# A vision-transformer layer with a matrix exponential: the count of squarings taken from the third and fourth powers

## The chip, the cores and the metric

The kernel runs on one core of one Trainium2 chip. The metric is the time of one execution on the device in microseconds (us), as the median of several runs. Its engines are named as in the profile: PE (TensorE), PEld (its weight load), DVE (VectorE), ACT (ScalarE), POOL (GpSimd), SP (SyncE, which here only issues DMAs).

## What is computed

32 images of 96x96 become 38 tokens of 256 features each (1216 rows). One attention layer with 16 heads follows, and then a feed-forward block with a mixture of experts. In the block, `expm` is the matrix exponential; its three arguments, the generators, are 256x256 and antisymmetric:

```python
logits = xn @ moe_gate_w + moe_gate_b
topw, topi = jax.lax.top_k(logits, K)             # K = 2 of E = 8 experts
h = _gelu(jnp.einsum('bsd,edh->ebsh', xn, ew1) + eb1[:, None, None, :])
eo = jnp.einsum('ebsh,ehd->ebsd', h, ew2) + eb2[:, None, None, :]
moe_out = jnp.einsum('ebsd,bse->bsd', eo, w_dense)
for i in range(NROT):                             # NROT = 3
    moe_out = moe_out @ expm(gens[i])
```

The entries of `gens` in the inputs are 8 x 0.5 x 0.02 x (g - g transposed) with g of unit normals, so their spread is 0.113. The largest sum of absolute values over a row or column of the three, worked out from the inputs, is 26.53.

## The kernel before, in words

The rows are cut into 11 tiles of 114 (three images each; the last has 76). Embedding, the projections and attention run tile by tile. Behind them a router gives every row its two experts, and the pairs of row and expert are packed into 26 slots of 128 rows, one expert to a slot. Then come the slots, and at the end a gather of the results with the last rotation, gate and store per tile.

**A slot j.** The program of each engine goes through the slots in a fixed order, written out by hand.

- POOL gathers the slot's 128 rows from memory by an indirect DMA into one of two buffers (`gather`, L445), and scatters the results (`scatter`, L450). Its loop (L465) runs: wait until the rows of slot j+2 are transposed, `gather(j+4)`, `scatter(j)` once DVE has written the results of slot j, then side work: a scale at L471 for j below 11, an add at L478 for j from 2 to 12, two diagonal matrices at L485 for j from 12 to 22.
- PE's loop (L1438) runs for slot j: `expert_of(j)` (a register loaded from SBUF), `turn_xs(j+2)` (transposes of the gathered rows, L1409), `hidden(j+1)` (first expert layer, L1422), at most one piece of the exponential, and `project(j)` (second layer, L1431).
- ACT evacuates the transposes (L624) and applies Gelu (L635). DVE adds the bias (`slot_step`, L1097) and so frees the bank for `project(j+2)` and starts `scatter(j)`. SP loads the first layer's weights, 512 KB a slot, three slots ahead (L322).

**The exponential.** `scale_generators` (L897, DVE) takes s as the larger of `SQUARINGS` = 4 and the exponent of (largest column sum of absolute values / 1.7), and multiplies the generators by 2^-s. PE makes the second, third and fourth powers of the three of them (`product`, L1362, evacuated by ACT at L603), and the transposes of the fourth (L1369, evacuated at L618). DVE builds a polynomial of degree 12 less the identity: `poly_first` (L1056) for generators 0 and 1 ahead of slot 0 and for 2 in slot 0, `poly_second` in slots 1 to 3 and `poly_third` in slots 4 to 6, each with a product of PE between. It is then squared s times: `turn_square` (four transposes), ACT's copy `keep_YT` (L648), `product`, and DVE's `square` (L1079, 2Y + Y squared). A loop behind slot 7 (`MORE_AT`) squares all three `more` = s - 3 times, and slots 8 to 16 (`SQ_AT`) carry one squaring each, which are the last three of every generator. In slots 17 and 19 (`E_AT`) the three results are multiplied together (`second`, `third`). The counts are set by one line:

```python
P0_AT, P1_AT, MORE_AT, SQ_AT, E_AT = 1, 4, 7, 8, (17, 19)
```

`link` on DVE puts a wait on each instruction's own completion behind it. `more` is loaded from SBUF into a register of PE at L1403, of ACT at L644 and of DVE at L1086, all ahead of slot 0.

Of the kernel before, what the change touches and what calls it, by code (L numbers as in the profile page):

```python
# [13 lines left out]
B, SEQ, D = 32, 38, 256  # L14
# [16 lines left out]
G = 3  # L31
SQUARINGS = 4
# [13 lines left out]
NCONST = 840  # L46
# [4 lines left out]
def vit_kernel(nc, patches, w_tok, w_qkv, w_o, w_pre, w1, w2, b2, gens, gens_t,  # L51
# [6 lines left out]
    with ctx:  # L58
# [3 lines left out]
        def sem(name):  # L62
            return ctx.enter_context(nc.semaphore(name))
# [64 lines left out]
        nrmi_sb = sb("nrmi_sb", 5, i32)  # L128
# [82 lines left out]
        var_set, root_set = sem("var_set"), sem("root_set")  # L211
        z_bounded = sem("z_bounded")
# [55 lines left out]
        P0_AT, P1_AT, MORE_AT, SQ_AT, E_AT = 1, 4, 7, 8, (17, 19)  # L268
# [220 lines left out]
        def _(act):  # L489
# [154 lines left out]
            more = act.value_load(nrmi_sb[0:1, 4:5], min_val=1, max_val=17)  # L644

# [8 lines left out]
            for j in range(NS - 2):  # L654
                keep_xsT(j + 2, j % 2)
                u = j - SQ_AT
                if 0 <= u < 3 * G:
                    keep_YT(3 * more + u + 1, u % G, 0)
                if j in E_AT:
                    n = E_AT.index(j)  # L660
                    act.wait_ge(e_turned, n + 1)
                    nc.scalar.activation(YT[n], bank[0][:, :], ACT.Copy).then_inc(e_evac, 1)
                gelu(j + 1, (j + 1) % 2, expert_of(j + 1))
                if j == 0:
                    act.wait_ge(d_z, 16 * NT)
                    nc.scalar.activation(h_sb[0:T, :].rearrange("p (t d) -> p t d", d=D),
                                         v_sb[0:T, 0:NT * PW].rearrange("p (t d) -> p t d", d=PW)[:, :, 0:D], ACT.Gelu).then_inc(abel_set, 1)
                if j == MORE_AT:
                    with act.Fori(0, more) as i:
                        for n in range(G):  # L670
                            keep_YT(3 * i + n + 1, n, MORE_BANK[n])
# [20 lines left out]
        def _(dve):  # L692
# [204 lines left out]
            def scale_generators():  # L897
# [6 lines left out]
                link(nc.vector.tensor_scalar(nrmi_sb[:, 4:5], nrmi_sb[:, 2:3], 1.0 - SQUARINGS, None, ALU.add))  # L904
# [136 lines left out]
            dve.wait_ge(n_scaled, 2)  # L1041
            c = [1.0]
            for k in range(1, 13):
                c.append(c[-1] / k)
# [26 lines left out]
            def poly_third(n):  # L1071
                stt(Y[n], A2[n], c[2], A[n])
                stt(Y[n], A3[n], c[3], Y[n])
                dve.wait_ge(p_made, G + n + 1)
                nc.vector.tensor_tensor(Y[n], Y[n], bank[0][:, :], ALU.add).then_inc(y_set, 1)
# [10 lines left out]
            more = dve.value_load(nrmi_sb[0:1, 4:5], min_val=1, max_val=17)  # L1086
# [36 lines left out]
            for j in range(NS):  # L1123
# [5 lines left out]
                if 0 <= u < 3 * G:  # L1129
                    square(3 * more + u + 1, u % G, 0)  # L1130
# [37 lines left out]
        def _(pe):  # L1168
# [234 lines left out]
            more = pe.value_load(nrmi_sb[0:1, 4:5], min_val=1, max_val=17)  # L1403

# [33 lines left out]
            for j in range(NS):  # L1438
# [3 lines left out]
                if 0 <= u < 3 * G:  # L1442
                    pe.wait_ge(s_kept_cr, 3 * more + G + u)
                    turn_square(bank[0], Y[u % G]).then_inc(s_turned, 1)
                if j in E_AT:
                    if j == E_AT[0]:
                        pe.wait_ge(s_kept_cr, 3 * more + 4 * G)
                    else:
                        pe.wait_ge(e_kept, 1)
                    turn_square(bank[0], Y[0]).then_inc(e_turned, 1)  # L1450
# [12 lines left out]
                if 0 <= u < 3 * G:  # L1463
# [7 lines left out]
                if j == MORE_AT:  # L1471
                    pe.wait_ge(y_set, G)
                    with pe.Fori(0, more) as i:
# [49 lines left out]
def _constants():  # L1523
# [13 lines left out]
    con[TLAST:, K_INV + NT - 1] = 100.0  # L1537
    con[:, K_SEG:K_SEG + E * NT] = (np.arange(E * NT) % NT != 0)
# [63 lines left out]
```

## Time and profile before

| | |
|---|---|
| median of 3 runs | 394.57 us (394.08 to 399.01) |
| the profiled execution | 394.72 us, its span 392.7 us |
| mean granted clock of PE over the span | 0.951 of full |
| PE, DVE, ACT, POOL busy | 88%, 55%, 45%, 39% |

The span runs from the first to the last instruction of the profiled execution; 2.0 us of its time lie outside. Start times in rows count from the start of the span.

### The profile page before, as it was taken

The numbers are of one execution on the slowest core, as the hardware profiler recorded it, in microseconds if no ns is written. First come the engines' busy times: TensorE is split into PE (matmuls) and PEld (weight loads), VectorE is DVE, ScalarE is ACT, GpSimd is POOL, SyncE is SP. The second block draws the span as 40 slices with busy tenths as digits, with TensorE's granted clock in tenths as the row PEclk, the third lists the DMA queues.
The fourth block names the chain that finished last, engine by engine and source line by source line (L and its number), as shares of the span: only waits on it lengthen the run. The fifth ranks groups of instructions, "written<-read, shape, count | busy, mean of one in ns | idle before, by whom it ended". The sixth has DMA issues, their size and how long they took to land.

```text
span 392.7 us, 6931 instructions
## 1 busy us (share of the span) xinstructions
PE 345.1 (88%) x2080; PEld 293.1 (75%) x2080; DVE 214.8 (55%) x581; ACT 178.5 (45%) x423; POOL 151.4 (39%) x168
## 2 busy tenths in 40 slices
PE   2998999769899999679986999999999999794894
PEld 2786454469788888556865899989999999693793
DVE  0237368797999999868785458421221123100175
ACT  1000354588998897335224844334434434341231
POOL 1002804050754663711041447653547446642000
PEclk9999899968999999969989999999999999989599
DMA  8741411133111100274222645523443444531442
GB/s 268 269 140 44 188 58 55 54 97 114 46 48 47 46 33 2 93 335 156 84 69 80 181 121 154 163 93 88 149 149 106 149 151 156 151 103 47 144 144 86
DMA packets 20544, 45.76 MB, mean 117 GB/s; under 512 B 2150, under 2 KB 12836, under 8 KB 20260
## 3 DMA queue, kind: packets, MB, share of 16 engines
q1 hardware_dynamic: 17732, 37.78, 29.1%
q0 software_dynamic: 2496, 6.82, 5.2%
q10 hardware_dynamic: 288, 0.81, 0.7%
q8 instruction: 14, 0.23, 0.3%
q14 instruction: 14, 0.11, 0.1%
HBM read 38.18 MB, written 7.22 MB: 116 GB/s over the span
## 4 chain that ended last, share of the span: by engine, by line
PE 75%; DVE 10%; issue 7%; DMA 3%; ACT 2%; POOL 1%; DVEq 0%; ACTq 0%; POOLq 0%; SPq 0%
PE banks L1422 11%; PE banks L1362 11%; PE banks L1431 10%; PE banks L1205 5%; PE banks L1175 5%; PE banks L1282 5%; PE banks L1258 4%; PE banks L1491 3%; PE banks L1300 3%; PE banks L1333 3%; PE banks L1501 2%; PE banks L1245 2%; PE banks L1191 2%; PE banks L1210 2%; PE banks L1231 2%
## 5 line engine op out<-in xcount | busy, mean ns | idle before, releaser
L1422 PE MATMUL banks<-qn_sb,w_sb 128*128 128x128 f32 x416 | 51.6, 278 | 1.0 <-ACT qn_sb L624 1.0
L624 ACT ACTIVATE qn_sb<-banks,col_sb 128x128 f32<-128x128 f32 x52 | 21.1, 458 | 66.1 <-PE banks L1409 66.1
L1431 PE MATMUL banks<-w_sb,sq_sb 128*128 x208 | 50.0, 385 | 0.3 <-ACT sq_sb L635 0.3
L1422 PEld LDWEIGHTS banks<-qn_sb,w_sb 128*128 128x128 f32 x416 | 49.2, 194 | 1.3 <-ACT qn_sb L624 1.2
L452 POOL DMA_INDIRECT y_rows<-pT_sb,sidx_sb x26 | 26.0, 999 | 56.7 <-DVE pT_sb L1097 55.5
L1431 PEld LDWEIGHTS banks<-w_sb,sq_sb 128*128 128x128 f32 x208 | 39.7, 194 | 5.7 <-issue 0.5
L1097 DVE TENSOR_TENSOR pT_sb<-banks,p_sb 128x256 f32<-128x256 f32 x26 | 11.0, 425 | 51.0 <-PE banks L1431 48.3
L635 ACT ACTIVATE sq_sb<-banks,col_sb 128x128 f32<-128x128 f32 x104 | 32.6, 369 | 12.9 <-PE banks L1422 10.8
L1175 PE MATMUL banks<-wtok_sb,patch_sb 128*114 128x256 f32 x132 | 30.4, 393 | 7.1 <-DMA wtok_sb<-in_w_tok 7.0
L446 POOL DMA_INDIRECT qn_sb<-z_rows,gidx_sb x26 | 27.4, 1054 | 21.1 <-PE banks L1409 14.1
L1175 PEld LDWEIGHTS banks<-wtok_sb,patch_sb 128*114 128x114 f32 x132 | 24.3, 186 | 12.8 <-DMA patch_sb<-in_patches 6.9
L541 ACT ACTIVATE kc_sb<-banks,col_sb 32x152 f32<-32x152 f32 x66 | 31.1, 471 | 2.6 <-PE banks L1245 1.5
L1079 DVE SCALAR_TENSOR_TENSOR p_sb<-p_sb,banks 128x512 f32<-128x512 f32 x12 | 8.3, 688 | 35.6 <-PE banks L1362 35.6
L829 DVE TENSOR_SCALAR kc_sb<-banks,col_sb 32x152 f32<-32x152 f32 x66 | 25.5, 423 | 3.7 <-PE banks L1245 3.2
L1362 PE MATMUL banks<-p_sb,wtok_sb 128*128 128x256 f32 x112 | 26.2, 380 | 0.0
L259 POOL TENSOR_TENSOR qn_sb<-qk_sb,wtok_sb 114x768 f32<-114x768 f32 x11 | 16.4, 1497 | 22.0 <-DVE wtok_sb L786 22.0
L411 POOL TENSOR_TENSOR att_sb<-p_sb 114x256 f32<-114x256 f32 x11 | 8.1, 738 | 41.8 <-DVE p_sb L864 41.8
L1205 PE MATMUL banks<-wqkv_sb,xT_sb 128*114 128x512 f32 x44 | 22.5, 635 | 0.2 <-ACT xT_sb L500 0.2
L1362 PEld LDWEIGHTS banks<-p_sb,wtok_sb 128*128 128x128 f32 x112 | 20.4, 190 | 2.3
L1258 PE MATMUL banks<-kc_sb,qd_sb 96*114 96x76 f32 x176 | 22.0, 274 | 0.0
L1258 PEld LDWEIGHTS banks<-kc_sb,qd_sb 96*114 96x114 f32 x176 | 22.0, 196 | 0.0
L532 ACT ACTIVATE qd_sb<-banks,col_sb 32x304 f32<-32x304 f32 x33 | 19.7, 598 | 4.1 <-PE banks L1231 3.8
(204 smaller groups left out, 668.8 us busy)
## 6 DMA issues: line engine op xcount, KB each, us to landing
w_sb<-in_w SPq DMA_DIRECT2D x26, 512.0 KB
w_sb<-in_w SPq DMA_DIRECT2D x1, 4096.0 KB, 12.6
patch_sb<-in_patches SPq DMA_DIRECT2D x11, 342.0 KB, 3.0
vrep_sb<-v_rows SPq DMA_DIRECT2D x33, 114.0 KB
qk_sb<-y_rows SPq DMA_DIRECT2D x10, 228.0 KB
v_rows<-v_sb SPq DMA_DIRECT2D x11, 114.0 KB
z_rows<-h_sb SPq DMA_DIRECT2D x11, 114.0 KB
out_rows<-h_sb SPq DMA_DIRECT2D x10, 114.0 KB
```

Source lines behind the costliest of these rows:

```text
L446: pool.indirect_dma_start(out=xs_sb[:, s * D:(s + 1) * D], out_offset=None, in_=z_dram, in_offset=bass.IndirectOffsetOnAxis(ap=gidx_sb[:, ...
L452: pool.indirect_dma_start(out=y_dram, out_offset=bass.IndirectOffsetOnAxis(ap=sidx_sb[:, j:j + 1], axis=0), in_=ys_sb[:, s * D:(s + 1) * D ...
L541: last = nc.scalar.activation(kc[:, :, a, :], bank[2][r, :].rearrange("p (n m) -> p n m", m=128)[:, :, c], ACT.Identity, scale=col_sb[r, C ...
L624: last = nc.scalar.activation(xsT_sb[:, (2 * s + c) * 128:(2 * s + c + 1) * 128], bank[1][:, c * 128:(c + 1) * 128], ACT.Identity, scale=c ...
L635: last = nc.scalar.activation(hidT_sb[:, s * HID + c * 128:s * HID + (c + 1) * 128], bank[2 + 2 * s + c // 2][:, (c % 2) * 128:(c % 2 + 1) ...
L829: last = nc.vector.tensor_scalar(kc[:, :, a, :], bank[3][r, :].rearrange("p (n m) -> p n m", m=128)[:, :, c], col_sb[r, C_GK + a:C_GK + a ...
L1175: last = nc.tensor.matmul(bank[2 + slot % 2][0:T, 0:D], patch_sb[:, (slot * FK + k) * T:(slot * FK + k + 1) * T], wtok_sb[:, k * D:(k + 1) ...
L1205: last = nc.tensor.matmul(bank[4 + s][0:T, :], xT_sb[:, (2 * s + k) * T:(2 * s + k + 1) * T], wqkv_sb[:, k * 3 * D:k * 3 * D + 2 * D], sta ...
L1258: last = nc.tensor.matmul(bank[4 + hf][0:T, n * 2 * SEQ:(n + 1) * 2 * SEQ], qd_sb[0:96, q0:q0 + T], kc_sb[0:96, k0:k0 + 2 * SEQ], start=Fa ...
L1362: last = nc.tensor.matmul(dst[:, m * D:(m + 1) * D], xT[:, k * D + m * 128:k * D + (m + 1) * 128], y[:, k * D:(k + 1) * D], start=(k == 0) ...
L1422: last = nc.tensor.matmul(bank[2 + 2 * s + c // 2][:, (c % 2) * 128:(c % 2 + 1) * 128], w1_sb[:, w0:w0 + 128], xsT_sb[:, (2 * s + k) * 128 ...
L1431: last = nc.tensor.matmul(bank[6 + s][:, 0:D], hidT_sb[:, s * HID + k * 128:s * HID + (k + 1) * 128], w2_sb[:, ds(e * 4 * D + k * D, D)], ...
```

## The change

It sets `SQUARINGS` to 2, so s stays what the column sums give if that is above 2. When the third and fourth powers are in SBUF, DVE sums the absolute values of their rows (six reductions of 128x512) and compares the largest of each with eight bounds, (1.7 / 2^q) to the third and to the fourth for q = 1 to 8. In slot 0, behind `turn_xs(2)`, PE multiplies the 16 comparisons with a matrix of ones, so that every partition has the counts over all 128. From them DVE takes t, the number of q for which neither power has a row at or over its bound, but at most s - 2, sets `more` = s - 2 - t + 1, and makes the coefficients of the polynomial as running products of 2^t / k. The polynomial is then that of 2^t times the scaled generator, which leaves s - t squarings: `more` of them in the loop, and one per generator in the slots. All of this comes before `poly_first(0)`. The pieces sit in other slots: `poly_second` in 2 to 4, `poly_third` in 5 to 7 (with one more DVE operation each), the loop behind slot 9, single squarings in slots 10 to 12, the products of the three in 14 and 16. `more` is now loaded into PE's and ACT's registers just ahead of the loop, and into DVE's ahead of `poly_first(0)`. The constants grow from 420 KB to 440 KB.

```diff
@@ -29,7 +29,8 @@
 EPS = 1e-5
 NEG = -1e30
 G = 3
-SQUARINGS = 4
+SQUARINGS = 2
+SHRINK = 8
 THETA = 1.7
 EXPM_LIMIT = 3.925724783138660 * 2.0 ** 17
 
@@ -43,7 +44,8 @@
 K_ID, K_MASK, K_LOW, K_ONE, K_IOTA, K_INV, K_SEG = 0, 128, 256, 384, 512, 640, 662
 K_TILE, K_ROW, K_DUMP = 750, 794, 795
 K_IMG, K_HEAD = 821, 824
-NCONST = 840
+K_RECIP, K_ZERO, K_BOUND = 840, 852, 864
+NCONST = 880
 NPART = 3
 Y_ROWS = 2 * NT * T + NS * 128
 
@@ -125,7 +127,8 @@
         wt_sb = sb("wt_sb", 4 * NT)
         z_sb = sb("z_sb", 4 * NT)
         nrm_sb = sb("nrm_sb", 16)
-        nrmi_sb = sb("nrmi_sb", 5, i32)
+        nrmi_sb = sb("nrmi_sb", 8, i32)
+        al_sb = sb("al_sb", 80)
 
         def tri(t_, k, w):
             return t_[0:T, ds(k * w, w)]
@@ -209,6 +212,7 @@
         x_made, x_kept, x_turned, x_evac, p_made, y_set = (
             sem("x_made"), sem("x_kept"), sem("x_turned"), sem("x_evac"), sem("p_made"), sem("y_set"))
         var_set, root_set = sem("var_set"), sem("root_set")
+        bound_set, counted, more_set = sem("bound_set"), sem("counted"), sem("more_set")
         z_bounded = sem("z_bounded")
         poly_set, stats_done = sem("poly_set"), sem("stats_done")
         s_made, s_kept_cr, s_turned, s_evac = sem("s_made"), sem("s_kept_cr"), sem("s_turned"), sem("s_evac")
@@ -265,7 +269,7 @@
             return not isinstance(t, int) or t >= n
 
         EARLY = 4
-        P0_AT, P1_AT, MORE_AT, SQ_AT, E_AT = 1, 4, 7, 8, (17, 19)
+        P0_AT, P1_AT, MORE_AT, SQ_AT, E_AT = 2, 5, 9, 10, (14, 16)
         MORE_BANK = (0, 4, 5)
 
         block = ctx.enter_context(nc.Block())
@@ -641,8 +645,6 @@
                 keep_xsT(j + 2, s)
                 gelu(j + 1, 1 - s, expert_of(j + 1))
 
-            more = act.value_load(nrmi_sb[0:1, 4:5], min_val=1, max_val=17)
-
             def keep_YT(done, n, b):
                 act.wait_ge(s_turned, done)
                 nc.scalar.activation(YT[n], bank[b][:, :], ACT.Copy).then_inc(s_evac, 1)
@@ -654,7 +656,7 @@
             for j in range(NS - 2):
                 keep_xsT(j + 2, j % 2)
                 u = j - SQ_AT
-                if 0 <= u < 3 * G:
+                if 0 <= u < G:
                     keep_YT(3 * more + u + 1, u % G, 0)
                 if j in E_AT:
                     n = E_AT.index(j)
@@ -666,6 +668,8 @@
                     nc.scalar.activation(h_sb[0:T, :].rearrange("p (t d) -> p t d", d=D),
                                          v_sb[0:T, 0:NT * PW].rearrange("p (t d) -> p t d", d=PW)[:, :, 0:D], ACT.Gelu).then_inc(abel_set, 1)
                 if j == MORE_AT:
+                    act.wait_ge(more_set, 1)
+                    more = act.value_load(nrmi_sb[0:1, 4:5], min_val=1, max_val=19)
                     with act.Fori(0, more) as i:
                         for n in range(G):
                             keep_YT(3 * i + n + 1, n, MORE_BANK[n])
@@ -901,7 +905,6 @@
                 link(nc.vector.tensor_scalar(nrmi_sb[:, 0:1], nrm_sb[:, 8:9].bitcast(i32), 23, None, ALU.logical_shift_right))
                 link(nc.vector.tensor_scalar(nrmi_sb[:, 1:2], nrmi_sb[:, 0:1], -126.0, float(SQUARINGS), ALU.add, ALU.max))
                 link(nc.vector.tensor_scalar(nrmi_sb[:, 2:3], nrmi_sb[:, 1:2], 20.0, None, ALU.min))
-                link(nc.vector.tensor_scalar(nrmi_sb[:, 4:5], nrmi_sb[:, 2:3], 1.0 - SQUARINGS, None, ALU.add))
                 link(nc.vector.tensor_scalar(nrmi_sb[:, 3:4], nrmi_sb[:, 2:3], -1.0, 127.0, ALU.mult, ALU.add))
                 link(nc.vector.tensor_scalar(nrm_sb[:, 9:10].bitcast(i32), nrmi_sb[:, 3:4], 23, None, ALU.logical_shift_left))
 
@@ -1038,10 +1041,32 @@
             nc.vector.tensor_scalar(R[3], R[0], 1.0, None, ALU.add).then_inc(hbs_set, 1)
 
 
-            dve.wait_ge(n_scaled, 2)
-            c = [1.0]
-            for k in range(1, 13):
-                c.append(c[-1] / k)
+            sums, top2 = al_sb[:, 0:12], al_sb[:, 12:14]
+            over, bad, tau = al_sb[:, 16:32], al_sb[:, 32:40], al_sb[:, 51:52]
+            c = [None] + [al_sb[:, 64 + k:65 + k] for k in range(12)]
+            for k, P in enumerate((A3, A4)):
+                for n in range(G):
+                    dve.wait_ge(x_kept, (k + 1) * G + n + 1)
+                    link(nc.vector.tensor_reduce(sums[:, 6 * k + 2 * n:6 * k + 2 * n + 2], P[n].rearrange("p (n c) -> p n c", c=D),
+                                                 AX.X, ALU.add, apply_absolute_value=True))
+            link(nc.vector.tensor_reduce(top2, sums.rearrange("p (k q) -> p k q", k=2), AX.X, ALU.max))
+            nc.vector.tensor_tensor(over.rearrange("p (k q) -> p k q", k=2), top2.unsqueeze(2).broadcast_to([128, 2, SHRINK]),
+                                    con_sb[:, K_BOUND:K_BOUND + 2 * SHRINK].rearrange("p (k q) -> p k q", k=2),
+                                    ALU.is_ge).then_inc(bound_set, 1)
+            dve.wait_ge(counted, 1)
+            link(nc.vector.tensor_reduce(bad, bank[0][:, 0:2 * SHRINK].rearrange("p (k q) -> p q k", k=2), AX.X, ALU.add))
+            link(nc.vector.tensor_scalar(bad, bad, 0.5, 1.0, ALU.is_ge, ALU.mult))
+            link(nc.vector.tensor_reduce(al_sb[:, 48:49], bad, AX.X, ALU.add))
+            link(nc.vector.tensor_scalar(al_sb[:, 48:49], al_sb[:, 48:49], -1.0, float(SHRINK), ALU.mult, ALU.add))
+            link(nc.vector.tensor_copy(nrmi_sb[:, 5:6], al_sb[:, 48:49]))
+            link(nc.vector.tensor_scalar(nrmi_sb[:, 6:7], nrmi_sb[:, 2:3], -float(SQUARINGS), None, ALU.add))
+            link(nc.vector.tensor_tensor(nrmi_sb[:, 5:6], nrmi_sb[:, 5:6], nrmi_sb[:, 6:7], ALU.min))
+            link(nc.vector.tensor_tensor(nrmi_sb[:, 6:7], nrmi_sb[:, 6:7], nrmi_sb[:, 5:6], ALU.subtract))
+            nc.vector.tensor_scalar(nrmi_sb[:, 4:5], nrmi_sb[:, 6:7], 1.0, None, ALU.add).then_inc(more_set, 1)
+            link(nc.vector.tensor_scalar(nrmi_sb[:, 7:8], nrmi_sb[:, 5:6], 127.0, None, ALU.add))
+            link(nc.vector.tensor_scalar(tau.bitcast(i32), nrmi_sb[:, 7:8], 23, None, ALU.logical_shift_left))
+            link(nc.vector.tensor_scalar(al_sb[:, 52:64], con_sb[:, K_RECIP:K_RECIP + 12], tau, None, ALU.mult))
+            link(nc.vector.tensor_tensor_scan(al_sb[:, 64:76], al_sb[:, 52:64], con_sb[:, K_ZERO:K_ZERO + 12], 1.0, ALU.mult, ALU.add))
             eye = con_sb[:, K_ID:K_ID + 128]
 
             def stt(out_, in0, k, in1):
@@ -1069,7 +1094,8 @@
                 add_eye(poly[n], c[4])
 
             def poly_third(n):
-                stt(Y[n], A2[n], c[2], A[n])
+                link(nc.vector.tensor_scalar(Y[n], A[n], c[1], None, ALU.mult))
+                stt(Y[n], A2[n], c[2], Y[n])
                 stt(Y[n], A3[n], c[3], Y[n])
                 dve.wait_ge(p_made, G + n + 1)
                 nc.vector.tensor_tensor(Y[n], Y[n], bank[0][:, :], ALU.add).then_inc(y_set, 1)
@@ -1083,7 +1109,8 @@
                 link(nc.vector.tensor_tensor_reduce(att_sb[0:T, 0:D], h_sb[0:T, t * D:(t + 1) * D], row_sb[0:T, R_GW:R_GW + D],
                                                     1.0, row_sb[0:T, R_GCB:R_GCB + 1], ALU.mult, ALU.add, z_sb[0:T, t:t + 1]))
 
-            more = dve.value_load(nrmi_sb[0:1, 4:5], min_val=1, max_val=17)
+            dve.wait_ge(more_set, 1)
+            more = dve.value_load(nrmi_sb[0:1, 4:5], min_val=1, max_val=19)
             dve.wait_ge(d_b, 16)
 
             def expert_of(j):
@@ -1126,7 +1153,7 @@
                 if P1_AT <= j < P1_AT + G:
                     poly_third(j - P1_AT)
                 u = j - SQ_AT
-                if 0 <= u < 3 * G:
+                if 0 <= u < G:
                     square(3 * more + u + 1, u % G, 0)
                 if j == E_AT[0]:
                     second()
@@ -1400,8 +1427,6 @@
             pe.wait_ge(experts_set, 1)
             pe.wait_ge(where_set, 1)
             pe.wait_ge(x_evac, G)
-            more = pe.value_load(nrmi_sb[0:1, 4:5], min_val=1, max_val=17)
-
             def turn_xs(j, s, turn):
                 pe.wait_ge(d_xs[s], 16 * (turn + 1))
                 pe.wait_ge(xsT_set, j)
@@ -1439,12 +1464,16 @@
                 u, e = j - SQ_AT, expert_of(j)
                 if j + 2 < NS:
                     turn_xs(j + 2, j % 2, j // 2 + 1)
-                if 0 <= u < 3 * G:
+                if j == 0:
+                    pe.wait_ge(bound_set, 1)
+                    nc.tensor.matmul(bank[0][:, 0:2 * SHRINK], con_sb[:, K_ONE:K_ONE + 128], al_sb[:, 16:32], start=True,
+                                     stop=True).then_inc(counted, 1)
+                if 0 <= u < G:
                     pe.wait_ge(s_kept_cr, 3 * more + G + u)
                     turn_square(bank[0], Y[u % G]).then_inc(s_turned, 1)
                 if j in E_AT:
                     if j == E_AT[0]:
-                        pe.wait_ge(s_kept_cr, 3 * more + 4 * G)
+                        pe.wait_ge(s_kept_cr, 3 * more + 2 * G)
                     else:
                         pe.wait_ge(e_kept, 1)
                     turn_square(bank[0], Y[0]).then_inc(e_turned, 1)
@@ -1460,7 +1489,7 @@
                     if n:
                         pe.wait_ge(y_set, n)
                     product(bank[0], A4T[n], poly[n]).then_inc(p_made, 1)
-                if 0 <= u < 3 * G:
+                if 0 <= u < G:
                     pe.wait_ge(s_evac, 3 * more + u + 1)
                     product(bank[0], YT[u % G], Y[u % G]).then_inc(s_made, 1)
                 if j in E_AT:
@@ -1470,6 +1499,8 @@
                 project(j, j % 2, e)
                 if j == MORE_AT:
                     pe.wait_ge(y_set, G)
+                    pe.wait_ge(more_set, 1)
+                    more = pe.value_load(nrmi_sb[0:1, 4:5], min_val=1, max_val=19)
                     with pe.Fori(0, more) as i:
                         for n in range(G):
                             pe.wait_ge(s_kept_cr, 3 * i + n + 1)
@@ -1535,6 +1566,9 @@
     con[:, K_ROW] = p
     con[:, K_DUMP:K_DUMP + NS] = 2 * NT * T + 128 * np.arange(NS) + p[:, None]
     con[TLAST:, K_INV + NT - 1] = 100.0
+    con[:, K_RECIP:K_RECIP + 12] = 1.0 / np.arange(1, 13)
+    for n in range(2):
+        con[:, K_BOUND + n * SHRINK:K_BOUND + (n + 1) * SHRINK] = (THETA / 2.0 ** np.arange(1, SHRINK + 1)) ** (n + 3)
     con[:, K_SEG:K_SEG + E * NT] = (np.arange(E * NT) % NT != 0)
     return con
 
```

## Rows read from the trace of the kernel before

**Rows 1.** The page, its head and the busy time of the engines.

```profile
span 392.7 us, 6931 instructions
...
PE 345.1 (88%) x2080; PEld 293.1 (75%) x2080; DVE 214.8 (55%) x581; ACT 178.5 (45%) x423; POOL 151.4 (39%) x168
```

**Rows 2.** Busy time by windows; behind the engines PE's clock, DMA share, GB/s.

```profile
320.00:340.00 20.00, 20.00 (x131) 18.42 (x130) 5.91 (x14) 9.36 (x27) 11.56 (x16) 1.00 0.49 150
```

**Rows 3.** Timeline, PE's `turn_xs` at the head of slots 9, 17, 20 and 21.

```profile
270.17 0.38 PE L1409 MATMUL banks<-con_sb,qn_sb 128*128 128x128 f32 x2
...
317.35 0.38 PE L1409 MATMUL banks<-con_sb,qn_sb 128*128 128x128 f32 x2
...
332.88 0.38 PE L1409 MATMUL banks<-con_sb,qn_sb 128*128 128x128 f32 x2
...
336.62 0.38 PE L1409 MATMUL banks<-con_sb,qn_sb 128*128 128x128 f32 x2
```

**Rows 4.** The instructions of L1079 (durations ns min/median/max).

```profile
L1079 DVE SCALAR_TENSOR_TENSOR p_sb<-p_sb,banks x12: 686/689/690, 260.2 to 315.8; 128x512 f32<-128x512 f32 x12
```

**Rows 5.** Chain that ended last, ahead of slot 0: start, length, what.

```profile
210.38 1.11 issue
```

**Rows 6.** Timeline of PE, `turn_xs(2)` in slot 0.

```profile
216.12 0.41 PE L1409 MATMUL banks<-con_sb,qn_sb 128*128 128x128 f32 x2 [0.99 <-ACT qn_sb L624]
```

**Rows 7.** The instructions of L792, a reduction of 128x512.

```profile
L792 DVE TENSOR_REDUCE nrm_sb<-p_sb x3: 668/676/677, 63.5 to 69.6; 128x2 f32<-128x512 f32 x3
```

**Rows 8.** Timeline of ACT: the last evacuation of a fourth power.

```profile
208.31 0.60 ACT L603 ACTIVATE qk_sb<-banks 128x512 f32<-128x512 f32 x1 [1.13 <-PE banks L1362]
```

**Rows 9.** Timeline of DVE: first and last of eleven linked 128x1 operations.

```profile
162.63 0.15 DVE L900 TENSOR_SCALAR nrm_sb<-nrm_sb 128x1 f32<-128x1 f32 x1
...
164.52 0.16 DVE L911 TENSOR_TENSOR nrm_sb<-nrm_sb 128x1 f32<-128x1 f32 x1
```

**Rows 10.** Timeline of DVE: `poly_first` of 0 and 1, then `slot_step(0)`.

```profile
205.56 0.43 DVE L1058 TENSOR_SCALAR qk_sb<-patch_sb 128x512 f32<-128x512 f32 x1 [1.55 <-ACT qk_sb L603]
...
211.69 0.29 DVE L1053 SCALAR_TENSOR_TENSOR qk_sb<-con_sb,qk_sb 128x128 f32<-128x128 f32 x1
220.74 0.42 DVE L1097 TENSOR_TENSOR pT_sb<-banks,p_sb 128x256 f32<-128x256 f32 x1 [8.75 <-PE banks L1431]
```

**Rows 11.** Timeline of POOL: `scatter(0)`, L471, `gather(5)`, and L471 in slot 1.

```profile
221.45 1.01 POOL L452 DMA_INDIRECT y_rows<-pT_sb,sidx_sb  x1 [3.19 <-DVE pT_sb L1097]
222.51 1.10 POOL L471 TENSOR_SCALAR hb_sb<-h_sb,rr_sb 114x256 f32<-114x256 f32 x1
223.78 1.28 POOL L446 DMA_INDIRECT qn_sb<-z_rows,gidx_sb  x1 [0.17 <-issue]
...
229.72 0.57 POOL L471 TENSOR_SCALAR hb_sb<-h_sb,rr_sb 114x256 f32<-114x256 f32 x1
```

**Rows 12.** Busy time by windows behind `gather(5)`, columns as in rows 2.

```profile
227.80:228.30 0.50, 0.50 (x5) 0.47 (x4) 0.33 (x1) 0.25 (x2) 0.00 (x0) 1.00 0.00 0
```

**Rows 13.** Timeline of PE: `turn_xs(5)` at the head of slot 3.

```profile
231.34 0.38 PE L1409 MATMUL banks<-con_sb,qn_sb 128*128 128x128 f32 x2
```

**Rows 14.** Timeline of DVE: `slot_step(19)` behind `third`.

```profile
335.20 0.42 DVE L1097 TENSOR_TENSOR pT_sb<-banks,p_sb 128x256 f32<-128x256 f32 x1 [0.84 <-DVE ywide_sb L1117]
```

**Rows 15.** Chain that ended last, around slot 22.

```profile
338.27 4.80 DMA qn_sb<-z_rows,gidx_sb
...
343.56 2.56 PE banks L1422 x16
346.12 2.61 PE banks L1431 x8
...
348.95 1.79 PE banks L1422 x16
```

**Rows 16.** Waits of PE in the slots: in total, times, longest.

```profile
PE banks L1409 <- DMA qn_sb<-z_rows,gidx_sb: 2.6, 1, 2.6
```

**Rows 17.** Busy time by windows behind that wait, columns as in rows 2.

```profile
344.00:347.00 3.00, 3.00 (x16) 2.82 (x15) 0.00 (x0) 1.66 (x6) 1.48 (x3) 0.56 0.30 81
```

## The prediction

> **What bounds the kernel now.** I read the page first: PE is busy for 88% of the span [rows 1]. A share over the whole span doesn't say what bounds the slots, where the change lies, so the windows come next. From 320 to 340 us PE is busy for all 20.00 us at full clock, while DVE has 5.91 and ACT 9.36 [rows 2]. So in the slots PE's work is the time. The timeline gives its size by the starts of `turn_xs`: from slot 9 to slot 17 it is 47.18 us for 8 slots with a squaring, 5.90 each; slot 20 carries no piece and takes 3.74 [rows 3]. A squaring of one generator thus costs PE 2.16. L1079 ran 12 times [rows 4]: four squarings of three generators, so s was 4 and `more` 1.
>
> Then the waits. In the slots PE waits once for a gather, 2.6 us [rows 16]. The chain around it shows why: DVE is late with `slot_step(19)` because `third` stands ahead of it and a register load follows, 0.84 idle [rows 14], so POOL is late with `scatter(19)` and with the gather behind it, which takes 4.80 from issue to landing [rows 15]. That line DVE, scatter, gather, PE is what the change can hit a second time. At the start, PE idles in pieces, and DVE sits idle for 8.75 us ahead of `slot_step(0)` [rows 10], which is cover for new work there.
>
> **How many squarings go.** The inputs give it. The largest column sum is 26.53, over 1.7 it is 15.6, so s stays 4 under the new minimum of 2. I worked out the powers of gens/16: the largest row sum of absolute values is 0.0524 in the third and 0.00914 in the fourth. The bounds are 0.0768 and 0.0326 at q = 2, and 0.0096 and 0.0020 at q = 3. So t = 2, which is also the cap s - 2. `more` is 1 again and one squaring per generator is left in slots: 2 instead of 4. Six squarings of one generator go: 6 x 2.16 = 13.0 us, all of it PE time in a stage where PE is never idle.
>
> **What comes back at the start.** Step by step in the time of the profile:
> - PE's load of `more` ahead of slot 0 goes. The chain has 1.11 "issue" there [rows 5]; about 1.0 of it should go. `turn_xs(2)` then starts at 216.12 - 1.0 = 215.1 [rows 6].
> - The reductions: six at 0.68 [rows 7]. DVE is free from about 204; the three over third powers are through by 206.1, the last over a fourth waits for its evacuation at 208.31 + 0.60 [rows 8] and ends at 209.6, the comparison by 210.1. PE asks for it at 215.3. That wait costs nothing, with 5 us to spare. DVE's idle 8.75 hides it.
> - The matrix product with ones is 128x16, which no row shows. Between nothing and a transpose pair (0.38, rows 6's kind); I take 0.2, and DVE sees it at 215.8.
> - Now 13 small operations in a chain. Linked 128x1 operations start (164.52 - 162.63)/10 = 0.19 apart [rows 9]: 2.5 us, to 218.3. Then DVE loads `more`, 0.8 by rows 14, to 219.1. In the kernel before these stood in idle time; here they lie on the line.
> - `poly_first` for two generators: from 205.56 to 211.98 it took 6.42 [rows 10]. The scalars now come from SBUF; I take the same price, and 10% more (0.6) as its other end. It ends at 225.5. Another register load shows with about 0.5: `slot_step(0)` starts at 226.0 instead of 220.74.
> - `scatter(0)` started 0.71 behind that, `gather(5)` 2.33 behind the scatter [rows 10, 11]: 229.0. In the kernel before, all packets had landed by 227.8 [rows 12], so that gather took at most 4.0; 3.5 is my estimate, 4.80 [rows 15] the upper end. It lands at 232.5.
> - PE needs it for `turn_xs(5)` at the head of slot 3. By then PE has done slots 0 to 2 with only one product of a polynomial (before: two), so it is there at about 228.4. It waits some 4 us, until 232.6. Before, slot 3 began at 231.34 [rows 13]. That is 1.3 later, and one product of 1.73 more is still owed (5.46 a slot with one product, less 3.74): 3.0 lost.
>
> `project(2)` needs `slot_step(0)` done, at 226.4; it comes to it at about 226.7. `poly_second(0)` is through at about 233, its product is due at 234.6. Nothing else is late on this line.
>
> **Smaller edits.** L471 behind `scatter(0)` took 1.10 while DVE was in the same kind of work, against 0.57 in slot 1 [rows 11]. I keep the long one; the short one would give 0.5 back. The Trainium skill (GPSIMD Engine Reference, section "1. Specifications") says that GpSimd contends with VectorE instructions of two SBUF inputs, of which `poly_first(2)` is made; by the rule the term stays, without it the sum would be 385.9.
> One DVE operation less in `scale_generators` gives 0.2. `poly_third` has one more per generator, 0.46, inside slots of 5.46 in which DVE has some 3.5: nothing, 1.4 without that cover. The register load ahead of the loop, in mid-work of all engines: PE loads one such register in every slot and slot 20 shows no gap, so nothing, 1.1 (rows 5) at most. ACT has the time until the first transposes of the loop. ACT loses six copies and DVE six operations, off the path. 20 KB more constants: nothing to 0.1.
> `third` now stands in slot 16, followed by slots without a piece as before: the same late scatter, the same wait of 2.6 and the same half clock, now at slot 19. But seven slots instead of four follow it, three of them still with side work on POOL: I add 0.2.
>
> **The sum.** -13.0 + 3.0 + 1.7 - 0.2 + 0.2 = -8.3. The profiled execution took 394.72, so 386.4. It stands 0.15 over the median, which makes no difference.
>
> **The rivals.**
> - *The line at the start isn't late.* If DVE's chain or the gather were some 4 us shorter, slot 3 begins without a wait: -13.0 - 1.0 + 0.2 = -13.8, that is 380.9. For it: 8.75 idle on DVE. Against: 6.42 of `poly_first` was done within that idle time's lead, and now all of it comes behind PE's product at 215.8.
> - *The wait comes, the clock stays.* 384.7. For it: the granted clock is held over the pieces of idle time around slot 0. Against: rows 15 to 17.
> - *The gathers bind more.* `gather(5)` takes 4.80: 1.3 later. And in slots 19 to 22 the ring from the end of slot j to `turn_xs(j+5)` is 0.3 (PE to DVE) + 0.71 + 1.0 + 1.2 + 0.2 + 4.8 = 8.2 against two slots of 3.74: 0.7 for every three slots, 1.2 in all with a part of a third. 386.4 + 2.5 = 388.9. For it: the 4.80 was in just such slots. Against: the half clock lengthens these slots and gives POOL time.
> - *The count doesn't shrink.* If the comparison finds a row over the bound at q = 1 (a fault in the count, or rounding far beyond the factor of 1.4 that I find between sum and bound), `more` is 3 and all 12 squarings stay, most in the loop. Then only the losses remain: 3.0 + 1.7 + 0.2 = +4.9, 399.6, slower than before. It decides at t: with t = 1 three squarings remain, -6.5 + 4.7 = -1.8; only t = 0 is slower. For it: a count over two engines in fp32. Against: the margins above.
>
> **How the numbers follow.** Forecast 386.4 with a chance of 0.45, the wait without the clock 0.2, late gathers 0.2, no wait 0.1, no shrinking 0.05. The range reaches from 381.5 (most of the case without a wait) to 390.5 (late gathers with the bounds of 0.6 for scalars and 1.1 for the register load). A measurement of this kernel can tell some 2%, 7.9 us, from no change; that is at 386.7, just over my forecast. Half of the forecast's share, most of the next and all of the case without a wait lie beyond it: faster 0.50, within 2% 0.47, slower 0.03 (the part of the last case that measures over 2%).
>
> **What would show it.** L1079 with 6 instructions, and slots 10 to 12 at 5.90. A wait of PE for a gather at slot 3 of 3 to 5 us, and one at slot 19 of 2.6. DVE's `slot_step(0)` some 10 us behind the matrix product with ones. A granted clock near 0.5 behind both waits. I'm wrong if `turn_xs(5)` finds its gather landed, if L1079 has other than 6, or if `bound_set` holds PE in slot 0.

## The result, and the profile after

| | before | after |
|---|---|---|
| median | 394.82 us (4 runs, 394.08 to 399.01) | 383.95 us (4 runs, 383.07 to 385.58) |
| profiled execution, span | 394.72, 392.7 | 384.60, 382.7 |
| granted clock of PE | 0.951 | 0.955 |

The ratio of after to before is 0.9708, with a 95% interval of 0.9631 to 0.9785: faster. Some executions of a program run at a lower granted clock and take over 1.5% longer than its fastest one; the ratios in this document leave them out. In a later set the same two programs gave 0.9742 (0.9696 to 0.9788). The forecast was 386.4, range 381.5 to 390.5; from profile to profile it was -8.3, and -10.1 was measured.

The head of the page after, its answer to [rows 1], and the instructions of the squaring (L1079 is now L1105):

```profile
span 382.7 us, 6792 instructions
...
PE 332.1 (87%) x2010; PEld 280.3 (73%) x2010; DVE 223.6 (58%) x598; ACT 175.5 (46%) x417; POOL 152.8 (40%) x168
```
```profile
L1105 DVE SCALAR_TENSOR_TENSOR p_sb<-p_sb,banks x6: 686/687/689, 272.8 to 293.0; 128x512 f32<-128x512 f32 x6
```

Six squarings are left of [rows 4]'s twelve, and PE's busy time fell by 13.0 us. The timeline of PE has `turn_xs` (now L1434) at the heads of slots 0 and 3 and the matmuls of `project(2)` (L1456); of DVE the first and last of the count's small operations (L1057, L1069), the first and last of `poly_first` for 0 and 1 and `slot_step(0)` (L1124):

```profile
215.85 0.41 PE L1434 MATMUL banks<-con_sb,qn_sb 128*128 128x128 f32 x2 [0.99 <-ACT qn_sb L628]
...
228.56 1.99 PE L1456 MATMUL banks<-w_sb,sq_sb 128*128 x8 [0.74 <-DVE pT_sb L1124]
...
234.29 0.44 PE L1434 MATMUL banks<-con_sb,qn_sb 128*128 128x128 f32 x2 [3.74 <-DMA qn_sb<-z_rows,gidx_sb]
```
```profile
216.43 0.17 DVE L1057 TENSOR_REDUCE al_sb<-banks 128x8 f32<-128x16 f32 x1 [5.83 <-PE banks L1469]
...
218.70 0.18 DVE L1069 TENSOR_TENSOR_SCAN al_sb<-al_sb,con_sb 128x12 f32<-128x12 f32 x1
...
219.93 0.49 DVE L1083 TENSOR_SCALAR qk_sb<-patch_sb,al_sb 128x512 f32<-128x512 f32 x1 [1.04 <-issue]
...
226.73 0.35 DVE L1078 SCALAR_TENSOR_TENSOR qk_sb<-con_sb,al_sb,qk_sb 128x128 f32<-128x128 f32 x1
227.87 0.42 DVE L1124 TENSOR_TENSOR pT_sb<-banks,p_sb 128x256 f32<-128x256 f32 x1 [0.79 <-issue]
```

The reader sees the predicted line: DVE idles 5.83 us until PE's product with ones, and from there everything is in a row, so `slot_step(0)` comes 7.13 us later than in [rows 10]. The chain that ended last goes on from it through POOL:

```profile
228.59 1.01 POOL y_rows L456
229.64 1.07 POOL hb_sb L475
230.89 3.36 DMA qn_sb<-z_rows,gidx_sb
234.29 0.44 PE banks L1434 x2
```

and the windows behind the wait at slot 3 and behind that at slot 19 have the clock at its full level (the eighth column), where [rows 17] had 0.56:

```profile
234.00:238.00 4.00, 3.71 (x25) 3.47 (x26) 3.06 (x7) 2.06 (x6) 2.75 (x4) 1.00 0.21 66
323.00:326.00 3.00, 3.00 (x23) 2.89 (x24) 0.17 (x1) 1.58 (x5) 2.67 (x4) 1.00 0.62 231
```

At slot 19 the wait is 1.43 where [rows 16] had 2.6: the gather before it took 3.62 us where [rows 15] had 4.80. Slots 20 and 21 (326.66 to 330.83, then to 334.77) take 4.17 and 3.94 instead of 3.74:

```profile
319.21 3.62 DMA qn_sb<-z_rows,gidx_sb
```
```profile
322.87 0.44 PE L1434 MATMUL banks<-con_sb,qn_sb 128*128 128x128 f32 x2 [1.43 <-DMA qn_sb<-z_rows,gidx_sb]
...
326.66 0.38 PE L1434 MATMUL banks<-con_sb,qn_sb 128*128 128x128 f32 x2
...
330.83 0.44 PE L1434 MATMUL banks<-con_sb,qn_sb 128*128 128x128 f32 x2 [0.27 <-issue]
...
334.77 0.44 PE L1434 MATMUL banks<-con_sb,qn_sb 128*128 128x128 f32 x2
...
338.56 0.38 PE L1434 MATMUL banks<-con_sb,qn_sb 128*128 128x128 f32 x2
```

The accounts close on these heads. Slot 3 began at 231.34 [rows 13] and begins at 234.29: 2.95 lost. From there to the last `turn_xs` (slot 23) it was 348.57 - 231.34 = 117.23 and is 338.56 - 234.29 = 104.27: 12.96 won. That is 12.96 of squarings, less 1.73 for the product that is still owed, plus 1.18 of shorter wait, plus 1.65 of clock, less 1.1 in small pieces (below). 2.95 - 12.96 = -10.0, as the spans have it; the last 0.1 of the 10.1 lies outside the span.

### The profile page after: what moved, and what is told of

Its sections match the earlier page's. It is cut to its first block, busy times and chain, and to the rows that moved or that the text cites. A ratio compares the mean times of both kernels' runs of the same rounds, so it can differ in the third digit from the quotient of the medians.

```text
span 382.7 us, 6792 instructions
## 1 busy us (share of the span) xinstructions
PE 332.1 (87%) x2010; PEld 280.3 (73%) x2010; DVE 223.6 (58%) x598; ACT 175.5 (46%) x417; POOL 152.8 (40%) x168
## 4 chain that ended last, share of the span: by engine, by line
PE 71%; DVE 13%; issue 7%; DMA 4%; ACT 2%; POOL 1%; DVEq 1%; POOLq 0%; ACTq 0%; SPq 0%
PE banks L1447 10%; PE banks L1456 9%; PE banks L1389 8%; PE banks L1232 5%; PE banks L1202 5%; PE banks L1309 5%; PE banks L1285 4%; PE banks L1522 3%; PE banks L1327 3%; PE banks L1360 3%; PE banks L1532 3%; PE banks L1272 2%; PE banks L1218 2%; PE banks L1237 2%; PE banks L1258 2%
## 5 line engine op out<-in xcount | busy, mean ns | idle before, releaser
L1456 PE MATMUL banks<-w_sb,sq_sb 128*128 x208 | 49.2, 380 | 0.8 <-DVE pT_sb L1124 0.7
L1456 PEld LDWEIGHTS banks<-w_sb,sq_sb 128*128 128x128 f32 x208 | 38.4, 190 | 6.0 <-issue 1.4
L1124 DVE TENSOR_TENSOR pT_sb<-banks,p_sb 128x256 f32<-128x256 f32 x26 | 11.0, 424 | 47.5 <-PE banks L1456 25.3
L450 POOL DMA_INDIRECT qn_sb<-z_rows,gidx_sb x26 | 28.7, 1103 | 20.1 <-PE banks L1434 13.2
L1309 PEld LDWEIGHTS banks<-vd_sb,pT_sb 114*114 114x114 f32 x132 | 17.8, 177 | 4.4 <-issue 3.8
L1309 PE MATMUL banks<-vd_sb,pT_sb 114*114 114x147 f32 x132 | 19.4, 287 | 1.4 <-ACT pT_sb L559 1.4
L1522 PE MATMUL banks<-patch_sb,qk_sb 114*128 114x114 f32 (+1 forms) x88 | 13.8, 313 | 7.6 <-DMA qk_sb<-y_rows 7.6
```

Of the source, the lines that this page charges most:

```text
L450: pool.indirect_dma_start(out=xs_sb[:, s * D:(s + 1) * D], out_offset=None, in_=z_dram, in_offset=bass.IndirectOffsetOnAxis(ap=gidx_sb[:, ...
L1309: last = nc.tensor.matmul(bank[6 + n // 3][0:T, n % 3 * IPT * VW:(n % 3 * IPT + w) * VW], pT_sb[0:w * SEQ, n * T:(n + 1) * T], vd_sb[0:w * ...
L1456: last = nc.tensor.matmul(bank[6 + s][:, 0:D], hidT_sb[:, s * HID + k * 128:s * HID + (k + 1) * 128], w2_sb[:, ds(e * 4 * D + k * D, D)], ...
```

## The experiments

Times of one program on different chips, and even the place of slot 0 in the span, differ by some 2 us and more. So each run is given by its ratio to the kernel before on its own chip, and by the distance in its profile from `turn_xs(2)` to the last `turn_xs`, slots 0 to 23, in us (before 348.57 - 216.12, after 338.56 - 215.85).

| run | ratio (95%) | slots 0 to 23 |
|---|---|---|
| before | 1 | 132.45 |
| after | 0.9708 (0.9631 to 0.9785) | 122.71 |
| after_again | 0.9742 (0.9696 to 0.9788) | 125.43 |
| no_count | 0.9615 (0.9562 to 0.9668) | 117.44 |
| step_first | 0.9780 (0.9734 to 0.9826) | 125.89 |
| no_shrink | 1.0101 (1.0067 to 1.0134) | 135.86 |
| chain_longer | 0.9896 (0.9853 to 0.9939) | 127.91 |
| third_behind | 0.9722 (0.9681 to 0.9762) | 121.34 |
| both_orders | 0.9720 (0.9673 to 0.9766) | 121.90 |
| constants_in | 0.9795 (0.9756 to 0.9834) | 124.23 |
| before_third_behind | 0.9894 (0.9857 to 0.9931) | 128.84 |
| pieces_later | 0.9615 (0.9557 to 0.9673) | 119.01 |

**no_count** prices all that the change adds.

```diff
-            sums, top2 = al_sb[:, 0:12], al_sb[:, 12:14]
...
-            link(nc.vector.tensor_tensor_scan(al_sb[:, 64:76], al_sb[:, 52:64], con_sb[:, K_ZERO:K_ZERO + 12], 1.0, ALU.mult, ALU.add))
+            c = [1.0]
+            for k in range(1, 13):
+                c.append(c[-1] * 4.0 / k)
```

> The changed kernel without the count on the chip: t is fixed to 2 (s to at least 4), the coefficients are constants, the six reductions, the comparison, PE's product with ones and the thirteen small operations are left out; slots and pieces stay where the change puts them. Theory (DVE's chain ahead of slot_step(0) is on the path by way of scatter(0) and gather(5)): the 3.74 us wait at the head of slot 3, the 0.74 us ahead of project(2) and 0.24 of PE's product go, so 384.0 - 4.7 = 379.3 us. Rival (later waits of POOL and the gathers would bind anyway and absorb it): 382.5 to 384.

PE's timeline has the heads of slots 2 and 3:

```profile
221.72 0.38 PE L1411 MATMUL banks<-con_sb,qn_sb 128*128 128x128 f32 x2
...
227.18 0.38 PE L1411 MATMUL banks<-con_sb,qn_sb 128*128 128x128 f32 x2
```

Slot 2 takes 5.46 and slot 3 starts without a wait. The distance is 5.27 less than after, of which 4.91 are made by the head of slot 3 (13.53 behind that of slot 0 instead of 18.44). The ratio says 0.9 to 1.3% less, about 4 to 5 us. The rival falls: the wait at slot 19 is 0.65 longer than in after (2.08), but slots 3 to 5 and 19 to 22 are otherwise 1.0 shorter, and nothing else takes it back.

**no_shrink** leaves every addition in and takes the gain away.

```diff
-        con[:, K_BOUND + n * SHRINK:K_BOUND + (n + 1) * SHRINK] = (THETA / 2.0 ** np.arange(1, SHRINK + 1)) ** (n + 3)
+        con[:, K_BOUND + n * SHRINK:K_BOUND + (n + 1) * SHRINK] = 0.0
```

> The changed kernel with all bounds at zero, so t = 0: every squaring stays (more = 3) and all that the change adds stays too. Theory (a squaring of one generator costs PE 2.18 us in the loop, and PE's work is the time): six of them back, 384.0 + 13.1 = 397.1 us, slower than before by some 2. Rival (part of the squarings' time lay in waits that the slots have anyway): 390 to 394.

The instructions of the squaring, and on PE the starts of two rounds of the loop:

```profile
L1105 DVE SCALAR_TENSOR_TENSOR p_sb<-p_sb,banks x12: 686/687/689, 272.4 to 305.8; 128x512 f32<-128x512 f32 x12
```
```profile
269.04 1.47 PE L1396 MATMUL banks<-con_sb,p_sb 128*128 128x128 f32 x12
...
275.61 1.60 PE L1396 MATMUL banks<-con_sb,p_sb 128*128 128x128 f32 x12
```

A round is 6.57, 2.19 a squaring; the distance grew by 13.15 against 13.1 expected. The ratio of 1.0101 makes it slower than before: what the change adds costs more than nothing, and the squarings alone pay for it.

**chain_longer** doubles the suspected cost.

```diff
+            for _ in range(16):
+                link(nc.vector.tensor_scalar(al_sb[:, 76:77], al_sb[:, 75:76], 1.0, None, ALU.mult))
```

> The changed kernel with 16 more linked 128x1 operations on DVE behind the scan of the coefficients, 3.0 us by 0.19 each. Theory: each us of that chain is a us of the whole: 387.0 us with the clock held; if the longer wait at slot 3 (6.8 us) brings the half clock, 1.7 more: 388.7. Rival (absorbed later): under 385.

Timeline of PE, `project(2)` and the head of slot 3, and the windows around and behind:

```profile
229.12 3.21 PE L1458 MATMUL banks<-w_sb,sq_sb 128*128 x8 [2.59 <-DVE pT_sb L1126]
...
234.80 0.69 PE L1436 MATMUL banks<-con_sb,qn_sb 128*128 128x128 f32 x2 [2.47 <-DMA qn_sb<-z_rows,gidx_sb]
```
```profile
229.00:232.00 3.00, 2.88 (x8) 2.07 (x8) 2.86 (x5) 0.00 (x0) 2.63 (x3) 0.62 0.12 44
234.00:240.00 6.00, 5.20 (x22) 4.92 (x23) 3.58 (x8) 2.06 (x6) 4.70 (x6) 0.50 0.20 70
```

Slot 3 begins 21.4 behind slot 0 instead of 18.44: 2.96 for 3.04 of chain. That is the theory, one for one. The clock fell to its lower level already behind the wait of 2.59 at `project(2)`, a wait for DVE and not for the gather, and stayed there until 240: slot 3 took 7.99 instead of 5.66, 2.3 more where 1.7 was expected. The distance ended 5.2 longer, and by the ratios the time is 1.5 to 1.9% longer, 6 to 7 us. The rival falls.

**step_first** moves `slot_step(0)` and `slot_step(1)` forward.

```diff
             poly_first(0)
-            poly_first(1)
...
-                if j == 0:
-                    poly_first(2)
+                if j < 2:
+                    poly_first(j + 1)
```

> The changed kernel with DVE's slot_step(0) ahead of poly_first(1) and slot_step(1) ahead of poly_first(2); nothing is left out. Theory: slot_step(0) starts one poly_first (3.55 us) earlier, near 224.3; gather(5) lands near 230.8, PE comes to slot 3 at about 229.8, so of the 4.5 us of waits about 1.0 is left: 380.5 us. Rival (the wait moves to gather(6) or to a product that waits for its polynomial): 383 to 384.

```profile
230.75 0.44 PE L1433 MATMUL banks<-con_sb,qn_sb 128*128 128x128 f32 x2 [1.56 <-DMA qn_sb<-z_rows,gidx_sb]
...
235.38 3.66 PE L1388 MATMUL banks<-qk_sb,kn_sb 128*128 128x256 f32 x8 [2.40 <-DVE qk_sb L1078]
```
```profile
235.00:239.00 4.00, 3.62 (x9) 2.97 (x10) 1.15 (x4) 0.00 (x0) 2.29 (x4) 0.57 0.42 154
```

PE's timeline shows the gather's wait shrink to 1.56, and slot 3 begins 3.2 earlier behind slot 0, as expected. But the product in slot 3 now waits 2.40 for DVE, which has the same work to do before it, and the clock fell behind that: slot 3 took 9.85 instead of 5.66, of which 2.40 is the wait and 1.8 the clock. The rival was right: the wait moved, and the whole became no shorter. Without the fall some 0.8 us of the 3.2 would have been left. DVE's work, not only its order, is on the line.

**pieces_later** draws the consequence: the same order, and no product in slot 3. It also has DVE's `slot_step(16)` ahead of `third()`, which third_behind below tries alone; both_orders below has the two orders without the move of the products.

```diff
-        P0_AT, P1_AT, MORE_AT, SQ_AT, E_AT = 2, 5, 9, 10, (14, 16)
+        P0_AT, P1_AT, MORE_AT, SQ_AT, E_AT = (2, 4, 5), 6, 9, 10, (14, 16)
```

> The changed kernel with slot_step(0) ahead of poly_first(1), slot_step(1) ahead of poly_first(2), slot_step(16) ahead of third(), and the products of poly_second in slots 2, 4 and 5 (in place of 2 to 4), of poly_third in 6 to 8, DVE's poly_second in 3 to 5. Nothing is left out. Theory (step_first lost what it won because the product in slot 3 waited 2.4 us for DVE): with no product in slot 3 PE waits some 1.6 us for gather(5) and for nothing else; from the head of slot 0 to that of slot 6 it is 1.73 for one product and 3.3 us net less than in the changed kernel, and 1.6 less at slot 19: 4.9 us less than after_again. Rival (the gathers or DVE's round bind in the slots behind): at most 2.5 us less.

The heads of slot 3 and the product of slot 4 on PE, and on DVE the last operation of its polynomial:

```profile
229.95 0.44 PE L1433 MATMUL banks<-con_sb,qn_sb 128*128 128x128 f32 x2 [1.55 <-DMA qn_sb<-z_rows,gidx_sb]
...
236.81 1.99 PE L1388 MATMUL banks<-qk_sb,kn_sb 128*128 128x256 f32 x8 [0.90 <-issue]
```
```profile
236.41 0.35 DVE L1078 SCALAR_TENSOR_TENSOR qk_sb<-con_sb,al_sb,qk_sb 128x128 f32<-128x128 f32 x1
```

The ratio is 0.9615 against 0.9742 for after_again on the same chip, 1.3% or 5.0 us less, and the two intervals don't meet. The median of all six times is 380.49 against 383.60, 3.1 less; they run from 377.78 at a granted clock of 0.961 to 385.38 at 0.937, and the four that the ratio counts have a median of 379.1. So the time agrees with the theory (4.9), but its parts don't. The heads of slots 0 to 9 lie 47.76 apart instead of 49.92: 2.2 won where 3.3 was expected. The product in slot 4 still waits 0.90, and starts 0.05 behind the end of DVE's last operation. At slot 19 the wait is 0.57 instead of 1.96. Together that is 3.6, between theory and rival. The distance fell by 6.4, mostly because after_again also had a fall of the clock (1.65) and a wait of 0.91 at slot 23, and this execution had neither. Against both_orders, which differs only in the slots of the polynomials' pieces, the distance is 2.9 less; there PE waited 2.37 for DVE in slot 3, and the clock fell behind that as in step_first. It is faster than both kernels.

**third_behind**, **both_orders** and **before_third_behind** look at the late wait.

```diff
+                slot_step(j, j % 2, j // 2 if j >= 2 else None)
                 if j == E_AT[1]:
                     third()
-                slot_step(j, j % 2, j // 2 if j >= 2 else None)
```

> The changed kernel with DVE's third() behind slot_step(16) instead of ahead of it; nothing is left out. Theory (the wait of 1.43 us at slot 19 comes from slot_step(16) being late by about 2 us): the wait goes, 384.0 - 1.4 = 382.6 us, and the 0.3 and 0.2 ahead of slots 21 and 22 may go as well: 382.0. Rival (the gather binds there anyway, POOL's round being as long as a slot without a piece): 383.5 or more.

> Both reorderings together: slot_step(0) ahead of poly_first(1), slot_step(1) ahead of poly_first(2), slot_step(16) ahead of third(). Nothing is left out. Theory (two separate waits, so the gains add): 384.0 - 3.5 - 1.7 = 378.8 us. Rival (the gathers take back what is gained): 380.5 or more.

> The kernel before with DVE's third() behind slot_step(19) instead of ahead of it; nothing is left out. Theory (its one gather wait of 2.6 us and the half clock behind it, 1.65 us, come from the late slot_step(19)): both go, 394.8 - 4.3 = 390.5 us. Rival (the half clock there comes from elsewhere, or the gathers bind anyway): 392.2 or more.

PE's timeline at slot 19 of third_behind, and at slot 22 of before_third_behind:

```profile
320.29 0.44 PE L1434 MATMUL banks<-con_sb,qn_sb 128*128 128x128 f32 x2 [0.36 <-DMA qn_sb<-z_rows,gidx_sb]
```
```profile
339.36 0.44 PE L1409 MATMUL banks<-con_sb,qn_sb 128*128 128x128 f32 x2 [0.55 <-DMA qn_sb<-z_rows,gidx_sb]
```

1.43 became 0.36 and 2.61 became 0.55. On the kernel before the edit gives 3.6 in the distance and 1.1% (0.7 to 1.4%) in time: the wait and the half clock behind it, as expected to within 0.7. On the changed kernel the distance falls by 1.37, but the ratios of third_behind and of after overlap, so in time nothing is shown. both_orders won nothing beyond it (0.9720 against 0.9722), for step_first's reason, so its rival was right.

**constants_in** takes one term out of the line.

```diff
-            c = [None] + [al_sb[:, 64 + k:65 + k] for k in range(12)]
+            c = [1.0]
+            for k in range(1, 13):
+                c.append(c[-1] * 4.0 / k)
```

> The changed kernel with the whole count and its chain kept, but the coefficients of the polynomials written as constants for t = 2 in place of operands from SBUF. Theory (scalar_tensor_tensor with a scalar from SBUF takes 0.79 us where it took 0.71 with a constant, and two poly_first lie on the path): 0.7 less, 383.3 us. Rival (the price of the operand is overlapped): 384.0.

In DVE's timeline three scalar_tensor_tensor take 2.15 here and, by the profile after, 2.32:

```profile
224.59 2.15 DVE L1075 SCALAR_TENSOR_TENSOR qk_sb<-qk_sb 128x512 f32<-128x512 f32 x3
```
```profile
220.45 2.32 DVE L1073 SCALAR_TENSOR_TENSOR qk_sb<-qk_sb,al_sb 128x512 f32<-128x512 f32 x3
```

The head of slot 3 is 17.77 behind that of slot 0, 0.67 less than after, as expected. The time isn't less (0.9795): 0.7 us is below what this comparison can tell. The profiled execution was the longest of its four, 389.34 us, and the clock fell in it during the wait of 3.75 at slot 3, so its 124.23 in the table holds 2.4 us of half clock. As a gain in time it stays open.

**after_again** is the changed kernel once more.

> The changed kernel itself, unaltered, beside the kernel before and in the same company as the next run: 2.9% less than before, and a wait of PE of 3.7 us at the head of slot 3. Theory (whether the half clock follows that wait differs from execution to execution of one program): its times lie up to 2 us apart, those with the lower granted clock being the longer ones.

Its waits of PE and the chain around slot 19:

```profile
PE banks L1434 <- DMA qn_sb<-z_rows,gidx_sb: 6.6, 3, 3.7
```
```profile
319.34 4.15 DMA qn_sb<-z_rows,gidx_sb
...
323.53 0.44 PE banks L1434 x2
323.97 2.56 PE banks L1447 x16
326.53 2.61 PE banks L1456 x8
```

The same program lost nothing behind 1.43 us of wait in one execution and 1.65 behind 1.96 in the other, while neither lost clock behind the 3.7 of slot 3. The two with the lowest clock (0.949) are its longest, 386.12 and 385.76; the other four lie between 382.44 and 383.80. So they lie up to 3.7 us apart, not 2, and the fall that differs was seen behind the late wait and not, as the theory had it, behind the one at slot 3.

## Why the prediction held, point by point

- *Squarings, -13.0.* Right, and the largest term: 12 to 6 instructions, no_shrink gives 13.15 back.
- *The line at the start, +3.0.* The mechanism was right (no_count, chain_longer), its size was short: slot 3 came 2.95 later, not 1.3, which makes 4.7. The terms: PE's removed load gave 0.3 at `turn_xs(2)`, not 1.0 (in this execution DVE's router work also ended 0.46 later), so DVE began at 216.43 instead of 215.8; its own load of `more` cost 1.04, not 0.8; `poly_first` twice 7.15, not 6.42, over even my upper end of 0.6 more; the second load 0.79, not 0.5. The gather took 3.36 against 3.5. POOL's L475 took 1.07, near the 1.10 that I kept. A wait of 0.74 at `project(2)` wasn't foreseen.
- *The clock, +1.7.* The step that failed. I took one fall behind one wait for a rule. No fall came behind 3.74 us here, and the fall behind the late wait, which I carried over as unchanged, wasn't there either. The runs show it to vary from execution to execution, so it belonged into the range and not into the sum. The Trainium skill's section (TensorE: Matmul & The Clock Gate, "HAM oscillation — how this bites in real kernels"), as I used it, has the half rate behind each such wait for a DMA. The traces agree behind the waits for a gather in after_again (1.96) and step_first (2.15), and disagree at slot 3 of after (3.74) and at slot 19 of no_count (2.08) and chain_longer (2.20).
- *The late wait, unchanged.* It was 1.43, not 2.61: its gather landed in 3.62 instead of 4.80, and nothing else differed. In before, after and the six other runs that leave `third` where it was, this wait is the gather's time less 2.18 or 2.19 (4.15 and 1.96 in after_again, 4.27 and 2.08 in no_count, 4.39 and 2.20 in chain_longer). 3.62 is the shortest of the eight, so part of the gain was luck. What makes a gather long isn't shown.
- *The small pieces, +0.2 and -0.2.* They came to 1.1: 0.7 in slots 19 to 22 (0.44 in slot 20 and 0.21 in slot 21), and 0.45 in slots 3 to 5, which took 5.66, 5.59 and 5.58 instead of 5.46. I had counted those as hidden. no_count has 5.46 there.
- *The sum.* Start 1.7 too low, clock 1.7 and 1.65 too high, late wait 1.2 too high, small pieces 1.1 too low: -8.3 + 1.7 - 1.7 - 1.65 - 1.2 + 1.1 = -10.05, against -10.1. Errors of 2.8 and of 4.55 us in opposite directions left 1.8, so the nearness of the total is partly luck. Of the 4.55, the late wait and the fall behind it differ between executions of one program: by after_again's ratio the time would be 384.6. The chance for a result beyond 2% was half, and the result lies there.

## What to carry to other kernels

Where one engine is never idle, work taken off it comes back at its full price, and that can be read from the distance of two heads in the timeline. A decision made on the chip costs the way through all engines that wait for it: price it along the line to the next transfer, with each register load (0.4 to 1.0 us of idle DVE here), not by busy time. When a wait is moved, ask which work on the same engine is next behind it; step_first lost all that it won, a little over half of it to the moved wait and the rest to the clock that fell behind it, and only moving the consumer as well (pieces_later) kept 2.2 us of it.

## What the runs showed of the hardware

- A fall of PE's granted clock to its lower level isn't tied to one length of wait. At slot 3 none came behind 3.68 to 3.81 us in four runs (after, after_again, no_shrink, third_behind), and one with 3.75 in constants_in. Behind the late wait it came with 1.96, 2.15 and 2.61 us (after_again, step_first, before) and not with 1.97, 2.05, 2.08 and 2.20 (constants_in, no_shrink, no_count, chain_longer), nor with 1.43 (after). Behind waits for DVE of 2.37, 2.40 and 2.59 (both_orders, step_first, chain_longer) it came each time. Each fall behind the late wait cost 1.65 us.
- The start of slot 0 goes with an early fall of the clock. Where it held between 36 and 46 us, slot 0 began at 213.2 to 214.7 us (six runs), and where it fell, at 215.4 to 216.1 (five runs), or at 220.1 in constants_in, which ran at half the clock from 80 to 100 us as well. The window 36 to 46 us of after_again, then of third_behind:

```profile
36.00:46.00 10.00, 7.87 (x25) 4.37 (x24) 4.37 (x15) 2.16 (x5) 6.87 (x11) 0.83 0.49 184
```
```profile
36.00:46.00 10.00, 7.87 (x30) 4.58 (x29) 6.08 (x18) 2.05 (x5) 6.87 (x11) 1.00 0.50 187
```

- `poly_third`'s scalar_tensor_tensor took between 0.93 and 1.64 us, the same in `poly_first` 0.75. The scalars from SBUF aren't the cause: with constants the six take as long (first line after, second constants_in). POOL's L475 and L482 run at the same time there; whether they stretch it wasn't tried:

```profile
L1073 DVE SCALAR_TENSOR_TENSOR p_sb<-qk_sb,al_sb,p_sb x6: 929/1284/1641, 249.4 to 260.0; 128x512 f32<-128x512 f32 x6
```
```profile
L1075 DVE SCALAR_TENSOR_TENSOR p_sb<-qk_sb,p_sb x6: 928/1286/1644, 254.6 to 265.1; 128x512 f32<-128x512 f32 x6
```
